# One core: x loaded already turned, and TensorE turns repeated means and deviations in its place

## The reference

```python
def _layernorm(x, axis=-1, eps=1e-05):
    m = jnp.mean(x, axis=axis, keepdims=True)
    v = jnp.var(x, axis=axis, keepdims=True)
    return (x - m) / jnp.sqrt(v + eps)
...
    x = x + jnp.tanh(g_xattn[0]) * _L0_xattn_ref(_layernorm(x, axis=-1), ctx_4096, ctx_4096, mask_BxSxS2_ff0, L0_xattn_wq, L0_xattn_wk, L0_xattn_wv, L0_xattn_wo, 0)
    x = x + jnp.tanh(g_ffn[0]) * _L0_ffn_ref(_layernorm(x, axis=-1), L0_ffn_route_w, L0_ffn_A, L0_ffn_Bw)
    return x
```

## Time and profile before

| | |
|---|---|
| median of 3 runs | 1052.81 us (1052.38 to 1053.01) |
| the profiled execution | 1052.97 us |
| its span | 1051.2 us |
| TensorE busy | 1041.9 us, 99% |
| VectorE busy | 872.2 us, 83% |
| ScalarE, GpSimd busy | 634.0 and 592.1 us |
| granted TensorE clock | 1.000 |

### The profile page before, as it was taken

The page is one execution under the profiler, slowest core; times in us unless marked ns, Lnnn a source line. Parts: engine busy times, 40 slices in busy tenths (PEclk is TensorE's granted clock), DMA queues, the critical chain, the costliest instruction groups (busy, mean ns, idle before and its releaser), DMA issues.

```text
span 1051.2 us, 19131 instructions
## 1 busy us (share of the span) xinstructions
PE 1041.9 (99%) x6663; PEld 865.3 (82%) x6663; DVE 872.2 (83%) x1423; ACT 634.0 (60%) x1112; POOL 592.1 (56%) x518
## 2 busy tenths in 40 slices
PE   9999999999999999999999999999999999999998
PEld 7888888877788888888888888888888888888786
DVE  7875766788888888888888899888887878787997
ACT  6554466676767666767665645556564655555653
POOL 4552379887878787878764533334343434444423
PEclk9999999999999999999999999999999999999999
DMA  7868966565765656565559844654454545443102
GB/s 264 266 223 303 401 221 250 160 261 212 252 214 184 222 180 211 194 199 204 166 221 392 279 144 158 190 182 149 153 175 135 180 145 171 163 147 131 46 26 81
DMA packets 106094, 206.40 MB, mean 196 GB/s; under 512 B 8848, under 2 KB 58640, under 8 KB 100112
## 3 DMA queue, kind: packets, MB, share of 16 engines
q1 hardware_dynamic: 105424, 204.40, 56.8%
q10 hardware_dynamic: 576, 0.79, 0.2%
HBM read 122.31 MB, written 82.84 MB: 195 GB/s over the span
## 4 chain that ended last, share of the span: by engine, by line
PE 89%; DVE 5%; POOL 2%; issue 1%; SPq 1%; DMA 0%; ACT 0%; DVEq 0%; POOLq 0%
PE attn L1003 31%; PE proj L928 26%; PE attn L870 7%; PE turned L870 4%; PE score L870 4%; PE attn L988 3%; PE score L950 3%; PE attn L990 3%; PE turned L963 3%; PE small L950 2%; PE proj L845 1%; DVE acc L1358 1%; POOL rot L1972 1%; PE proj L950 1%; DVE o_s L1346 1%
## 5 line engine op out<-in xcount | busy, mean ns | idle before, releaser
L1003 PE MATMUL attn<-wo_s,o_s 128*128 128x512 f32 x1524 | 375.0, 395 | 0.6 <-DVE o_s L1346 0.5
L928 PE MATMUL proj<-xB,wq_s 128*128 128x512 f32 x1344 | 334.4, 391 | 0.1
L1003 PEld LDWEIGHTS attn<-wo_s,o_s 128*128 128x128 f32 x1524 | 280.8, 188 | 58.5 <-DVE o_s L1346 1.5
L928 PEld LDWEIGHTS proj<-xB,wq_s 128*128 128x128 f32 x1344 | 251.3, 188 | 51.8 <-issue 0.7
L1972 POOL TENSOR_TENSOR rot<-rot,tab 128x512 f32<-128x512 f32 x110 | 162.6, 1478 | 146.6 <-ACT rot L1691 146.4
L1246 DVE TENSOR_TENSOR q_r<-q_r,tab 128x512 f32<-128x512 f32 x127 | 114.2, 899 | 1.5 <-ACT x_third L1691 1.4
L1346 DVE TENSOR_TENSOR o_s<-attn,o_s 128x512 fp32r<-128x512 f32 x127 | 82.5, 685 | 33.9 <-ACT o_s L1740 33.9
L1712 ACT ACTIVATE copies<-proj 128x512 f32<-128x512 f32 x96 | 57.4, 598 | 80.7 <-PE proj L928 80.6
L1740 ACT ACTIVATE o_s<-attn 128x512 fp32r<-128x512 f32 x127 | 69.3, 597 | 57.1 <-PE attn L990 57.1
L1358 DVE SCALAR_TENSOR_TENSOR acc<-attn,gates_t,acc 128x512 f32<-128x512 f32 x127 | 94.9, 748 | 10.2 <-PE attn L1003 7.9
L1972 POOL TENSOR_TENSOR rot_third<-rot_third,tab 128x512 f32<-128x512 f32 x40 | 61.6, 1540 | 57.9 <-ACT rot_third L1691 55.0
(11 more groups left out here) (280 smaller groups left out, 1735.2 us busy)
## 6 DMA issues: line engine op xcount, KB each, us to landing
wq_kept<-wq_s SPq DMA_DIRECT2D x16, 1792.0 KB, 6.6
wq_s<-wq_kept SPq DMA_DIRECT2D x16, 1792.0 KB, 7.7
v_kept<-vst SPq DMA_DIRECT2D x64, 256.0 KB, 4.2
v_s<-v_kept SPq DMA_DIRECT2D x128, 128.0 KB, 5.0
wo_kept<-wo_s SPq DMA_DIRECT2D x32, 512.0 KB, 6.5
wo_s<-wo_kept SPq DMA_DIRECT2D x32, 512.0 KB, 5.5
k_kept<-kst SPq DMA_DIRECT2D x32, 256.0 KB, 2.1
wq_raw<-in_wq SPq DMA_DIRECT2D x16, 512.0 KB, 7.9
```

The lines of the kernel that those rows point to most:

```text
L928: last = e.matmul(dst[:, :], wq_s[:, b % 2, A, s, kt, :], xB[:, B, mv, kt, :], start=(first and kt == 0 and m == 0), stop=(kt == 1 and m = ...
L1003: last = e.matmul(out_bank(k, bp)[:, :], o_s[:, s, bp, h, :], wo_s[n % WO_SLOTS][:, m, :], start=(h == 0 and i == 0), stop=(h == GROUP - 1 ...
```

## The change

x is now given in a second layout, `xT`, with the model dimension on the partitions (128 rows of 512 numbers a tile, as before), and loaded where the turning used to leave it. The statistics still need rows by token, so each tile of x is also loaded as before, into `x_rows0` and `x_rows1`, which lie where the mask and the route weights go later. These two are therefore loaded at jobs 48 and 53 in place of 12 and 14.

Mean and inverse deviation of a tile are two columns of `x_stats`. TensorE takes each as a stationary operand, repeated 128 times, and transposes it (`spread_stats`), four transposes for a pair into one bank, so that each PSUM row holds the numbers of the 128 tokens. VectorE then subtracts and multiplies with two tensor_tensors a tile (`x_norms_end`), reading that bank. ScalarE's copies back are gone. The places: statistics at jobs 8, 10, 13, 16, 19, 21, 23, 25 (`X_STATS`); for a pair beside job n turning at n + 2, norm at n + 3, sums by GpSimd at n + 5, splits at n + 6. The special cases for the last pair are gone. Loads of x and stores of xB move. Some semaphores are shared by two uses; the wide steps keep their order.

```diff
-XB_STORE = (24, 26, 28, 30, 32, 34, 36)
-X_TURN, X_COMBINE, X_SPLIT = 3, 4, 5
+XB_STORE = (26, 27, 28, 30, 31, 33, 35)
+X_TURN, X_NORM, X_COMBINE, X_SPLIT = 2, 3, 5, 6
...
-X_FETCH = [6, 8, 9, 14, 28, 29, 31, 33]
+X_FETCH = [7, 8, 10, 15, 27, 28, 19, 22]
+
+
+
+X_STATS = (8, 10, 13, 16, 19, 21, 23, 25)
+ROWS_FETCH = (6, 7, 9, 12, 15, 18, 20, 22)
+MASK_FETCH, ROUTED_FETCH = 48, 53
...
+        def x_stat(w, which):
+
+            at = (2 * w[3] + which) * P
+            return proj[x_number(w) % 2][:, at:at + P].unsqueeze(1).to_broadcast([P, KT, P])
...
-            return x_tiles[w[1] * HALF_TILES + w[3] * CHUNK_TILES + w[2]]
+            return xT[x_tile(w)]
...
+            def fetch_rows(no):
+                if no >= 2:
+                    e.wait_ge(ln_moments, CHUNKS * (no - 1))
+                for c, w in enumerate(X_PAIRS[X_ORDER[no]]):
+                    e.dma_start(x_rows(no)[:, c, :], x_tiles[x_tile(w)]).then_inc(rows_here(no, c)[0], 16)
...
-            def turn_x(pair):
-                e.wait_ge(ln_done, NORM_NO[X_PAIRS[pair][1]] + 1)
+            def spread_stats(pair):
+
+                no = X_NO[pair]
+                e.wait_ge(ln_rstd, CHUNKS * (no + 1))
+                if no >= 2:
+                    e.wait_ge(x_normed, CHUNKS * (no - 1))
                 for c, w in enumerate(X_PAIRS[pair]):
-                    if X_NO[pair]:
-                        e.wait_ge(x_copied, 2 * X_NO[pair] - 1 + c)
-                    turn(proj[c], 0, x_place(w), cols=KT).then_inc(x_turned, 1)
+                    for which in range(2):
+                        at = (2 * c + which) * P
+                        last = e.transpose(proj[no % 2][:, at:at + P],
+                                           x_stats[:, NORM_NO[w], which:which + 1].to_broadcast([P, P]), ident)
+                last.then_inc(stats_spread, 1)
...
-            def x_norms_begin(pair):
+            def x_norms_begin(no):
+                for c, w in enumerate(X_PAIRS[X_ORDER[no]]):
+                    e.wait_ge(*rows_here(no, c))
+                    norm_begin(w, x_rows(no)[:, c, :])
+
+            def x_norms_end(pair):
+                e.wait_ge(stats_spread, X_NO[pair] + 1)
                 for w in X_PAIRS[pair]:
                     e.wait_ge(*raw_here(w))
-                    norm_begin(w, x_place(w))
-
-            def x_norms_end(pair):
+                    e.tensor_tensor(x_by_token(w), x_by_token(w), x_stat(w, 0), ALU.subtract).then_inc(x_less_mean, 1)
                 for w in X_PAIRS[pair]:
-                    norm_end(w, x_place(w), x_place(w))
+                    e.wait_ge(x_less_mean, NORM_NO[w] + 1)
+                    e.tensor_tensor(x_by_token(w), x_by_token(w), x_stat(w, 1), ALU.mult).then_inc(x_normed, 1)
...
-            def x_copies(pair):
-                for c, w in enumerate(X_PAIRS[pair]):
-                    e.wait_ge(x_turned, 2 * X_NO[pair] + c + 1)
-                    e.activation(x_place(w), proj[c][:, :], ACT.Copy).then_inc(x_copied, 1)
```

More of the change, by code:

```diff
@@ L319, in wo_low_step, with build @@
     return 3 if j == 1 else j
-def build(nc, x, ctx, mask, g_attn, g_ffn, wq, wk, wv, wo, routed_w, lora_b, table, out):
+def build(nc, x, xT, ctx, mask, g_attn, g_ffn, wq, wk, wv, wo, routed_w, lora_b, table, out):
     x_tiles = x.rearrange("b s d -> (b s) d").rearrange("(t p) d -> t p d", p=P)
@@ L419, in build @@
         kv_banks = [score, turned] + attn
-        table_in, gates_in, routed_in = sem("table_in"), sem("gates_in"), sem("routed_in")
-        mask_in = [sem(f"mask_in{c}") for c in range(CHUNKS)]
+        table_in, gates_in = sem("table_in"), sem("gates_in")
+        mask_place_in = [sem(f"mask_place_in{c}") for c in range(CHUNKS)]
+        routed_place_in = [sem(f"routed_place_in{c}") for c in range(CHUNKS)]
         acc_in = [sem(f"acc_in{t}") for t in range(HALF_TILES)]
@@ L640, in fetch_mask @@
                     e.wait_ge(masked, 4 * (KV_HEADS - 1) + 2 * c + 2)
-                e.dma_start(mask_sb[:, c], mask[index]).then_inc(mask_in[c], 16)
+                else:
+                    e.wait_ge(ln_moments, X_TILES)
+                e.dma_start(mask_sb[:, c], mask[index]).then_inc(mask_place_in[c], 16)
             def fetch_acc(half, t):
@@ L1208, in norm_begin @@
                 i = n % 4
-                if n >= 4:
-                    e.wait_ge(ln_done, n - 3)
+                here = x_stats[:, n, :] if norm[0] == "x" else moments[:, i, :]
+                if n >= X_TILES + 4:
+                    e.wait_ge(ln_done, n - X_TILES - 3)
+                elif n >= 4:
+                    e.wait_ge(ln_rstd, n - 3)
                 e.bn_stats(stats[:, i, :], src).then_inc(ln_stats, 1)
                 e.wait_ge(ln_stats, n + 1)
-                e.bn_aggr(moments[:, i, :], stats[:, i, :]).then_inc(ln_moments, 1)
+                e.bn_aggr(here, stats[:, i, :]).then_inc(ln_moments, 1)
                 e.wait_ge(ln_moments, n + 1)
-                e.tensor_scalar(var_eps[:, i:i + 1], moments[:, i, 1:2], LN_EPS, None, ALU.add).then_inc(ln_var, 1)
+                e.tensor_scalar(var_eps[:, i:i + 1], here[:, 1:2], LN_EPS, None, ALU.add).then_inc(ln_var, 1)
             def norm_end(norm, dst, src):
@@ L1424, in _ @@
             for n in range(len(JOBS)):
-                if n in X_BESIDE and n < X_LAST:
-                    x_norms_begin(X_BESIDE[n])
+                if n in X_STATS:
+                    x_norms_begin(X_STATS.index(n))
                 if n == SCORES_AFTER:
@@ L1461, in _ @@
                     raw_low(w)
-                if n - X_SPLIT in X_BESIDE and n + 1 != X_LAST:
+                if n - X_SPLIT in X_BESIDE:
                     x_lows(X_BESIDE[n - X_SPLIT])
@@ L1775, in _ @@
                         copy_product(*p)
-                if n - X_TURN in X_BESIDE and JOBS[n][0] == "v":
-                    x_copies(X_BESIDE[n - X_TURN])
                 finish_job(n)
@@ L1915, in inverse_std @@
                 e.wait_ge(ln_var, n + 1)
-                if n >= 4:
-                    e.wait_ge(ln_done, n - 3)
-                e.tensor_tensor(rstd[:, i:i + 1], var_eps[:, i:i + 1], power[:, :], ALU.pow).then_inc(ln_rstd, 1)
+                if n >= X_TILES + 4:
+                    e.wait_ge(ln_done, n - X_TILES - 3)
+                here = x_stats[:, n, 1:2] if norm[0] == "x" else rstd[:, i:i + 1]
+                e.tensor_tensor(here, var_eps[:, i:i + 1], power[:, :], ALU.pow).then_inc(ln_rstd, 1)
             def raw_low(w):
@@ L1962, in combine_x, with x_norms @@
                 e.tensor_tensor(t4, c0[:, right], t2, ALU.subtract).then_inc(x_combined, 1)
-            def x_norms(pair):
-                for w in X_PAIRS[pair]:
+            def x_norms(no):
+                for w in X_PAIRS[X_ORDER[no]]:
                     inverse_std(w)
```

86 lines of the change are left out of this document (48 added, 38 removed).

## The result

The changed kernel takes 1064.16 us (median, 1063.79 to 1064.48), the kernel before 1052.91 us in runs beside it on the same chip. The ratio is 1.0109, with a 95% interval of 1.0097 to 1.0121. The forecast was 1062.0.

What follows compares the result with a forecast made beforehand. The prediction took TensorE's stream and its holes to bound the kernel. Losses of 8.4 (VectorE), 2.0 (stores) and 2.0 (first product) less 3.2 saved gave +9.2 us, so 1062.0 us, range 1051.5 to 1068.

Steps and rivals of the forecast that it cites:

- What bounds the kernel: Whole span: TensorE's instruction stream plus its holes; a microsecond off the stream counts if the other engines keep up.
- TensorE saves 3.2: Turning of pairs: four transposes instead of eight take 0.49 us where 0.89 was, 3.2 us saved for eight pairs.
- Rival (e): Turning of pairs: the repeated column loads slower, so nothing is saved; 1065 us, chance 0.10 shared with the added-loads rival.
- The norm costs 2.4: VectorE's norm of a pair: four tensor_tensors reading PSUM at 0.60 us each, 2.4 us, bounds 2.0 and 5.0.
- VectorE's backlog, 8.4: VectorE up to job 25: 53.3 us of work plus 10.2 idle in 55.0 of room, TensorE losing 8.4 us.
- the walk: Job-by-job reckoning of the four engine queues with assumed durations, giving when VectorE ends each job and TensorE needs its bank.
- Stores of blocks, 2.0: At job 39: tighter block stores delay the release of job 35 to 125.0, costing TensorE 2.0 us, bounds 0 and 5.
- First product, 2.0: At the first product: rounds of pairs 4 to 7 and the weights end late, costing 2.0 us, bounds 0 and 4.
- (a): VectorE's queue: it keeps up and TensorE's gain stays whole, 1049.6 us; chance 0.15.
- (b): VectorE's queue: only its smallest loss, 3.5 us, with neither stores nor rounds late; 1053.1 us, no change; chance 0.09.
- (d): Input loads: 4 MB added for rows delays the splits for job 12 or 16, another 2 to 4 us, 1065; shared chance 0.10.

Runs made afterwards that it cites:

- transposes twice: Changed kernel with late statistics, sums behind the sin product, block stores spread, and each transpose of a mean or deviation made twice: 1053.32 us.
- statistics late: Changed kernel with the statistics of pairs 4 to 7 at jobs 26, 28, 30, 32 instead of 19, 21, 23, 25, their rows loaded accordingly: 1056.03 us.
- both: Changed kernel with statistics of pairs 4 to 7 late and GpSimd's sums of pairs 2 and 3 behind the sin product: 1054.15 us.
- both, stores apart: Changed kernel with late statistics, sums behind the sin product, and block stores spread to jobs 26, 28, 30, 32, 34, 35, 36: 1051.59 us.
- no scaling: Changed kernel without the multiplication by the inverse deviation, two of the four instructions of a norm: 1057.70 us.
- the first three runs: Changed kernel with statistics of pairs 4 to 7 late (1056.03 us), with sums of pairs 2 and 3 behind the sin product (1058.07), and with these together (1054.15).
- sums behind sin: Changed kernel with GpSimd's sums of pairs 2 and 3 behind the sin product of jobs 20 and 24, their splits one job later: 1058.07 us.
- stores apart only: Changed kernel with only the block stores moved, to jobs 26, 28, 30, 32, 34, 35, 36: 1063.44 us.

## Why the prediction was right, step by step

**What bounds the kernel.** Right: TensorE's stream and its holes. Every microsecond of the difference up to the product is found as a hole or a saving: 11.0 (jobs 23 to 30) + 0.5 (job 39) + 1.8 (transposes behind job 40) + 0.9 (product: 1.1, less the 0.2 of the earlier trace rows) - 3.4 - 0.25 = 10.5 to 10.6, against 10.47 measured. All are distances from start to start; the 0.25 is the earlier start of job 2 (12.00 against 12.25), which differs from profile to profile and which the forecast had not.

**TensorE saves 3.2.** Measured 3.4: the transposes themselves came out as forecast (0.36 for four), and the price on the job behind is 0.11 instead of 0.09. What made the saving larger was that before a pair cost 0.89 and now 0.47, where 0.49 was taken. Rival (e), a slow repeated column, is excluded by "transposes twice". By the Trainium skill (TensorE: Matmul & The Clock Gate, Back-to-back issue gap), with some 81 ns a matmul in a stream of loads and matmuls, the saving would have been 2.6, an estimate. The runs have 0.09 to 0.11 us for one.

**The norm costs 2.4.** Measured 2.39, and never held back: the rows at 79.58 and 80.78 run at this pace although GpSimd makes a sin product from 79.67 to 80.97. Beside such a product L1221 of the kernel before took 2.54 for two instructions. The Trainium skill's rule on the shared port (SBUF — State Buffer), by which an instruction with one input in SBUF is not locked out, is borne out by this, and so is its other side, by which two inputs in SBUF are: a lower part of that form, 0.42 us elsewhere, took 1.51 beside a sin product.

```profile
64.35 1.51 DVE L1291 TENSOR_TENSOR xB<-x_near,xB 128x256 fp32r<-128x256 f32 x1
```

**VectorE's backlog, 8.4.** The mechanism and the places held, the size did not: 11.0. This is the term that was mis-sized most. The waits stand where the walk had them (jobs 25, 26, 28, 29) and at job 24 besides. The sum is set by when job 25 is through: the walk had 96.1, and VectorE's next instruction starts at 97.98, 1.9 us later. Job 20 accounts for 0.7 of it: the lower halves ahead of it were held up by GpSimd (the 1.51 us above, for 0.42), while the idle time at job 20 was 3.67 instead of 4.0. Job 24 accounts for the rest: the walk had VectorE idle 2.8 us there behind sin, but it idled 3.71 behind ScalarE, which stood 6.96 us in its own queue for the sums and the upper halves before it came to the split that VectorE wanted first:

```profile
89.68 0.63 ACT L1690 ACTIVATE xB<-combined 128x512 fp32r<-128x512 f32 x1 [6.96 <-POOL combined L1999]
...
91.35 0.61 ACT L1710 ACTIVATE ctxT<-far_raw 128x512 fp32r<-128x512 f32 x1
```

Besides, TensorE begins 0.06 us after the write's end, not at VectorE's next start (98.12 against 97.98: 0.14), it wanted the banks 0.4 us earlier than walked (73.71 for job 24 instead of 74.1: 0.25 from the start, the rest from the pairs turned), and it lost 0.17 more at job 30. 1.9 + 0.1 + 0.4 + 0.2 = 2.6, which is the difference of 8.4 and 11.0.

**Stores of blocks, 2.0.** This term was right only in its size, and by luck. The release of job 35 was forecast at 125.0 and came at 125.38, by two errors that cancel: the stores of job 25 went out at 98.09 instead of 96.7, and the release followed 27.3 us behind them instead of 28.3.

```profile
125.38 0.60 ACT L1747 ACTIVATE vst<-attn 128x512 fp32r<-128x512 f32 x1 [6.50 <-DMA v_kept<-vst]
```

TensorE, however, came to job 39 2.0 us later than walked because of the backlog, so it lost only 0.5 there (0.20 of it idle). Nor does the wait at job 39 grow where the backlog is gone: "statistics late", "both" and "both, stores apart" have none, and the most is the 0.57 us of "no scaling". The wait that the stores do cause was not in the walk. ScalarE's copy of job 37 waits 3.18 us for the store of job 33, VectorE's queue is held behind it, and so the norm of pair 4 ends at 134.03 (the walk had 133.9). The four transposes behind job 40 write the bank that this norm reads, so TensorE waits for its end. The walk had the right end and never asked who needs it before the product does: 1.8 us here, 1.35 to 1.6 in the first three runs, nothing once the stores are apart. The size of about 2 us came from a place that the prediction did not name.

**First product, 2.0.** Measured 0.9: 1.1 from start to start, less the 0.2 that was there before; within its bounds of 0 and 4. The lower halves of pair 4 ended at 142.25 as walked (142.5), the three rounds took 5.6 us each instead of 5.2, and the product started at 163.45 where 162.5 was forecast. That would have cost more, but TensorE itself came to it 2.1 us later than walked, mostly through the 1.8 of the transposes. Taken together the two ends of this path gave 2.7 us where 2.0 was forecast.

**The sum.** Forecast +9.2, measured +10.8 on the profiled executions: 2.6 more for VectorE, 0.8 less for the stores and the way to the product (3.2 for 4.0), 0.5 more saved (3.7 for 3.2), 0.3 less between the product and the span's end, and 0.6 more outside the span. That last part is not explained. It is there in each kernel with the change whatever its order; the change has one more input tensor and other semaphores, and neither was tried by itself.

**Rivals.** (a) 1049.6, VectorE keeps up: excluded for the order as written, and almost reached (1050.2) once three orders were altered. (b) needed the sums not to hold back sin: "sums behind sin" is that case, and it gave 1058, not 1053. The amount of work alone still costs a wait of 3.41, about the 3.5 of this rival, but (b) had neither the clock behind that wait (1.7) nor the wait of the transposes (1.5 idle) nor that at the product (0.6). (d) No split came late: no wait of the jobs before 24 is in TensorE's list.

## What to carry to other kernels

Where the bounding engine waits for nothing, look at the slack of whoever releases it before adding work there, and count forced idle time with the work: here 55 us of room held 53 us of work but not the order that put 3.3 us of sums ahead of a 1.3 us product that the next step wants. Work that nobody needs for ten jobs belongs behind the crowded stretch, even if it was put early to be safe. But its loads move with it: rows for the late statistics then came between the stores of blocks, landed late, and cost 1.4 to 1.8 us at job 36. Before such a wait is put down to an old cause, read what the engine that releases it was itself waiting for.

## What the runs showed of the chip

TensorE's granted clock fell in the middle of the losses. After idle times of 1.08, 1.72 and 1.77 us at jobs 24, 25 and 26 it stood at 0.69 on the mean through job 26 (length, busy us of PE, PEld, DVE, ACT, POOL, clock, DMA share, GB/s):

```profile
84.51:88.52 4.01, 4.01 (x12) 3.18 (x13) 3.65 (x9) 0.00 (x0) 2.50 (x4) 0.69 0.44 163
```

That is between the two levels of 1.2 and 2.4 GHz, so it was at the lower for a part of the job, and made it 1.3 us longer (2.72 of 4.01 is 0.68). It cost nothing in the end, since job 28 waits for VectorE anyway: in the profile of "stores apart only", with nearly the same idle times ahead, TensorE ran job 26 at a clock of 1.00 and waited 3.10 us at job 28 instead of 1.50:

```profile
92.99 3.06 PE L912 MATMUL score<-ctxT,wk_s 128*128 128x512 f32 x12 [3.10 <-DVE kst L1307]
```

The same idle time does not always take clock. Behind the 3.10 us above the next job ran at 1.00, while behind 3.11 us in "no scaling" it ran 4.61 us long, and behind the 3.41 us of "sums behind sin" job 26 stood at 0.65:

```profile
82.70:86.91 4.21, 4.21 (x12) 3.35 (x13) 4.07 (x10) 0.00 (x0) 2.70 (x3) 0.65 0.94 334
```

There no job up to 39 waits for VectorE afterwards, so the 1.7 us are lost as far as the transposes behind job 40, which wait 1.5 us for the norm of pair 4. Whether that wait would have been longer with the full clock, no run shows.
